# An LSTM with an adapter on one core: projection by quadrants, bias by matmuls, and the adapter's weight in 32 chained transfers

## The chip, the cores and the metric

One core of a Trainium2 chip runs the kernel. The metric is the device time of one execution in microseconds; three runs of the kernel before gave 603.7, 605.48 and 606.89, median 605.48.

## The reference

The input x has 16 sequences of 256 tokens with 256 features, all in 32-bit floats. An LSTM layer comes first, with residual:

```python
xz = einsum('ntd,dk->ntk', x, Wx) + b            # k = 4 gates of 256: i, f, o, g
z = xz_t + prev_h @ Wh                           # 256 steps, one after the other
next_c = sigmoid(f) * prev_c + sigmoid(i) * tanh(g)
next_h = sigmoid(o) * tanh(next_c)               # h0 = cond, c0 = 0
x = x + hs
```

Then an adapter, with residual, whose low-rank weights differ for each sequence and come from cond:

```python
c = layernorm(cond) * gamma + beta
h = gelu(c @ W1 + bias1)
w = h @ W2 + bias2                               # 16 x 8192; W2 is 256 x 8192, 8 MB
a1, b1, a2, b2 = split(w)                        # each 16 x 256 x 8
mid = gelu(x @ base_down + (x . a2) . b2)
out = x + mid @ base_up.T + (mid . b1) . a1
```

## The kernel before

Time is cut into 32 blocks of 8 steps. A block is 128 tokens (16 sequences by 8 steps), which fill the 128 partitions. For each block SP loads x (`load_x`), TensorE transposes it (`transpose_x`), ScalarE copies it to SBUF times two (`evacuate_x`), TensorE multiplies it with Wx in eight pieces (`project`: four column quarters of 256, two halves of the contraction), VectorE adds the bias on the way from PSUM to `proj` (`evacuate_projection`), and four SP DMAs move `proj` to `seed` (`load_seed`), so that the four quadrants of 32 partitions each hold a quarter of the hidden units for the 16 sequences, for every step of the block. This runs two blocks ahead of the recurrence.

A step: ScalarE copies the seeds into the PSUM banks z0, z1 and z_o (`seed_bank`, `seed_o`); TensorE adds h times Wh, with the 16 sequences as weights, four quadrants side by side (line 677); VectorE turns 32 by 32 blocks, ScalarE takes tanh, VectorE forms the cell and the hidden state, which is already transposed and is the next step's stationary operand. In the gaps TensorE does the projection of block k + 2 and the adapter of the block before.

Up to block 2 a planner by step, `make_weights`, puts the making of the adapter's weights between: W1 and the transposes of base_up in steps 2 to 5 of block 0, then W2 in 16 pieces, one a step from step `W_FIRST` = 7 on (line 606), its result added to bias2 by VectorE (line 882) and spread by POOL's DMAs (`place_w`, line 975) to w_tmp, b_t and a_t, of which w_tmp is transposed (line 618) in block 2. W2 is loaded in four transfers of 2 MB into three tiles (`load_w2`, line 276): the first at the start, two in block 0, the last in block 1, when its tile is free. bias2 is loaded by POOL, broadcast to 16 partitions in each quadrant.

Each engine works in program order and waits on semaphores. SP's order matters here: a DMA that stands behind a wait is not issued before the wait ends. In the projection before, the columns go gate by gate, so that one evacuation holds one gate for all quadrants, and a seed DMA, which takes one quadrant, needs all four. The bias b is spread to all partitions at the start by one-row matmuls (line 634); four matmuls on zeros run before (line 625).

Of the kernel before, what the change touches and what calls it, by code (L numbers as in the profile page):

```python
# [20 lines left out]
ALU = mybir.AluOpType  # L21
ACT = mybir.ActivationFunctionType
# [3 lines left out]
G = 4  # L26
P = 128
# [14 lines left out]
W_FIRST = 7  # L42
# [12 lines left out]
WARM_UP = 4  # L55


def lstm_adapter(nc, x, cond, Wx, Wh, b, base_up, base_down, gamma, beta, W1, bias1, W2, bias2, out):
    ctx = ExitStack()
    with ctx:  # L60
# [6 lines left out]
        def sem(name):  # L67
# [5 lines left out]
        ones = sb("ones", [P, P])  # L73
# [3 lines left out]
        b_row = sb("b_row", [1, G * H])  # L77
# [23 lines left out]
        w2 = {q: w2_tiles[n % 3] for n, q in enumerate(QUARTERS)}  # L101
        w_bias = sb("w_bias", [P, 4, W_COLS])
# [39 lines left out]
        consts_made = sem("consts_made")  # L142
        zeroed = sem("zeroed")
        w_loaded = {n: sem(f"{n}_loaded") for n in
                    ("wx_if", "wx_og", "wh", "b", "down", "up", "ln", "cond", "w1")}
        w2_loaded = [sem(f"w2_loaded{q}") for q in range(4)]
        w_bias_zeroed, w_bias_loaded = sem("w_bias_zeroed"), sem("w_bias_loaded")
# [38 lines left out]

        def gate_cols(t, gate):

            quadrants = t[:, :].rearrange("p (j n) -> p j n", n=ZW)
            if gate == 2:  # L190
                return quadrants[:, :, NM * GC:ZW].rearrange("p j (m c) -> p m j c", c=C)
            place = {0: 0, 1: 1, 3: 2}[gate]
            return quadrants[:, :, 0:NM * GC].rearrange("p j (m g c) -> p g m j c", m=NM, c=C)[:, place]
# [48 lines left out]
        def _(sp):  # L242
# [6 lines left out]
            def load_seed(f):  # L249
# [23 lines left out]
            w2_q = W2.rearrange("(k p) (q n) -> q p k n", p=P, q=4)  # L273
# [5 lines left out]
            sp.dma_start(b_row[:, :], b.rearrange("(a n) -> a n", a=1)).then_inc(w_loaded["b"], 16)  # L279
            load_cols(wx, Wx, 0, 0, 2 * H, "wx_if")  # L280
            load_cols(wx, Wx, 2 * H, 2 * H, 2 * H, "wx_og")
            sp.dma_start(c_in[:, :], cond).then_inc(w_loaded["cond"], 16)
            load_cols(wh, Wh, 2 * H, 3 * H, H, "wh")
            load_cols(wh, Wh, 0, 0, 2 * H, "wh")
            load_cols(wh, Wh, 3 * H, 2 * H, H, "wh")
# [9 lines left out]
            load_w2(QUARTERS[0])  # L295
# [30 lines left out]
        def _(act):  # L326


            act.wait_ge(zeroed, 1)
# [10 lines left out]
            def seed_bank(buf, s, m):  # L340

                act.activation(z_bank[m][:, 0:GC], seed[buf][:, s, GC * m:GC * (m + 1)], ACT.Copy)\  # L342
                   .then_inc(seeded[m], 1)

            def seed_o(buf, s):
                act.activation(o_bank[:, 0:OC], seed[buf][:, s, NM * GC:ZW], ACT.Copy).then_inc(seeded_o, 1)  # L346
# [14 lines left out]

            def make_weights(k, s):
# [11 lines left out]
                if k == 2 and s in (0, 4):  # L374
# [5 lines left out]
            def double_g(t, lo, ready):  # L380
# [628 lines left out]
```

## Time and profile before

| | |
|---|---|
| median of three runs | 605.48 us |
| profiled execution | 607.91 us, span of its instructions 605.7 |
| TensorE busy | 586.7 us (97%) |
| VectorE, ScalarE, GpSimd busy | 83%, 63%, 8% |
| mean granted TensorE clock | 0.994 |
| DMA | 39.74 MB, mean 66 GB/s |

The span is the time from the first to the last instruction of one profiled execution; the run's own time is 2.2 us longer. PE is TensorE, PEld its loading of weights, DVE VectorE, ACT ScalarE, POOL GpSimd, SP the engine that issues most DMAs. A 32-bit matmul of the program shows as two instructions. The spans of matmuls overlap, since they are pipelined: the distance of two starts says more than a duration.

### The profile page before, as it was taken

Reading aid. Unit: us, or ns where it says so; the run is one execution under the profiler, and the core shown is the slowest. Engines: PE = TensorE matmul, PEld = TensorE weight load, DVE = VectorE, ACT = ScalarE, POOL = GpSimd, SP = SyncE. Lnnn points to the kernel's source line nnn. Section 1 sums busy time; section 2 is a strip of 40 time slices with the busy share of each in tenths; the row PEclk is TensorE's granted clock in tenths of the full one; section 3 lists DMA queues with packets and bytes.
Section 4 is the critical chain, followed back from the end, with each engine's and each line's share of the span. In section 5 each row is a group of like instructions: output and inputs, shape, how many; then the busy total and the mean of one; then the engine's idle time right before and its main releaser. Section 6 shows DMA issues by size and latency. Waiting matters only on the chain.

```text
span 605.7 us, 34198 instructions
## 1 busy us (share of the span) xinstructions
PE 586.7 (97%) x14092; PEld 437.7 (72%) x14092; DVE 501.5 (83%) x2805; ACT 384.6 (63%) x2154; POOL 49.7 (8%) x96
## 2 busy tenths in 40 slices
PE   8698999999999999999999999999999999999997
PEld 5564567777777777777777777777777777777885
DVE  2577888888888888888888888888888888888873
ACT  1365566666666666666666666666666666666673
POOL 5001320000000000000000000000000000000000
PEclk9799999999999999999999999999999999999999
DMA  7889340232323113233311232322133233113201
GB/s 193 218 219 311 68 56 15 36 55 56 56 56 52 32 31 56 55 56 56 56 32 28 56 55 56 55 47 39 29 57 55 55 56 53 34 30 45 56 21 29
DMA packets 32142, 39.74 MB, mean 66 GB/s; under 512 B 3906, under 2 KB 29810, under 8 KB 30963
## 3 DMA queue, kind: packets, MB, share of 16 engines
q1 hardware_dynamic: 31282, 36.51, 30.3%
q8 instruction: 112, 1.84, 1.4%
q0 software_dynamic: 704, 1.05, 1.2%
q14 instruction: 44, 0.35, 0.2%
HBM read 16.05 MB, written 4.19 MB: 33 GB/s over the span
## 4 chain that ended last, share of the span: by engine, by line
PE 95%; issue 1%; DMA 1%; DVE 1%; POOL 1%; SPq 0%; ACT 0%; POOLq 0%; ACTq 0%
PE z L677 36%; PE x_bank L481 19%; PE z_o L677 9%; PE aux L507 8%; PE out_bank L531 7%; PE aux L492 3%; PE aux L459 3%; PE out_bank L563 2%; PE aux L514 2%; PE out_bank L606 1%; DMA seed<-proj 1%; PE out_bank L552 1%; PE x_bank L552 1%; DMA x_nat<-in_x 0%; PE x_bank L507 0%
## 5 line engine op out<-in xcount | busy, mean ns | idle before, releaser
L677 PE MATMUL z<-wh,h_t 128*16 128x96 f32 x8160 | 235.3, 249 | 3.5 <-issue 3.1
L677 PEld LDWEIGHTS z<-wh,h_t 128*16 128x16 f32 x8160 | 153.2, 96 | 109.5 <-DVE h_t L855 79.6
L830 DVE STREAM_TRANSPOSE z<-z 128x96 f32<-128x96 f32 x512 | 152.8, 299 | 73.3 <-PE z L677 47.6
L404 ACT ACTIVATE gates<-z 128x48 f32<-128x48 f32 x512 | 108.1, 211 | 122.6 <-DVE z L830 122.3
L481 PE MATMUL x_bank<-wx,x_t 128*128 128x256 f32 x512 | 156.3, 393 | 0.5 <-ACT x_t L336 0.5
L342 ACT ACTIVATE z<-seed 128x96 f32<-128x96 f32 x512 | 127.0, 248 | 5.8 <-DMA seed<-proj 5.8
L677 PE MATMUL z_o<-wh,h_t 128*16 128x64 f32 x4080 | 104.9, 219 | 0.1
L840 DVE SCALAR_TENSOR_TENSOR prod<-gates 128x32 f32<-128x32 f32 x512 | 98.7, 193 | 0.0
L481 PEld LDWEIGHTS x_bank<-wx,x_t 128*128 128x128 f32 x512 | 81.3, 197 | 5.9 <-issue 1.5
L677 PEld LDWEIGHTS z_o<-wh,h_t 128*16 128x16 f32 x4080 | 80.0, 97 | 0.6 <-issue 0.5
L346 ACT ACTIVATE z_o<-seed 128x64 f32<-128x64 f32 x256 | 58.4, 228 | 19.3
L952 POOL TENSOR_TENSOR xp<-x_t,h_t 128x128 f32<-128x128 f32 x60 | 30.4, 530 | 483.2 <-DVE h_t L855 449.1
L410 ACT ACTIVATE gate_o<-z_o 128x32 f32<-128x32 f32 x256 | 50.6, 198 | 27.1 <-DVE z_o L834 1.7
L834 DVE STREAM_TRANSPOSE z_o<-z_o 128x64 f32<-128x64 f32 x256 | 65.9, 257 | 0.2
L416 ACT ACTIVATE z_o<-z 128x16 f32<-128x16 f32 x256 | 43.0, 168 | 25.8 <-DVE z L845 0.4
L766 DVE TENSOR_TENSOR proj<-x_bank,b_all 128x256 f32<-128x256 f32 x128 | 54.1, 422 | 6.2 <-PE x_bank L481 6.0
L845 DVE SCALAR_TENSOR_TENSOR z<-prod 128x16 f32<-128x16 f32 x256 | 46.7, 182 | 8.7
L850 DVE SCALAR_TENSOR_TENSOR gates<-prod 128x32 f32<-128x32 f32 x256 | 47.2, 185 | 0.0
L416 ACT ACTIVATE tanc<-tanc 128x16 f32<-128x16 f32 x256 | 45.6, 178 | 0.2
L855 DVE SCALAR_TENSOR_TENSOR h_t<-gate_o,z_o 128x16 f32<-128x16 f32 x256 | 43.7, 171 | 0.2
L855 DVE SCALAR_TENSOR_TENSOR h_t<-gate_o,tanc 128x16 f32<-128x16 f32 x256 | 43.7, 171 | 0.0
L507 PE MATMUL aux<-xp,down 128*128 128x128 f32 x232 | 43.3, 289 | 0.0
(125 smaller groups left out, 518.9 us busy)
## 6 DMA issues: line engine op xcount, KB each, us to landing
seed<-proj SPq DMA_DIRECT2D x128, 128.0 KB, 4.4
w<-in_L_cond_W SPq DMA_DIRECT2D x4, 2048.0 KB, 10.6
x_nat<-in_x SPq DMA_DIRECT2D x32, 128.0 KB, 4.3
out<-y_nat SPq DMA_DIRECT2D x32, 128.0 KB, 4.2
wx<-in_L_cond_Wx SPq DMA_DIRECT2D x2, 512.0 KB, 4.9
wh<-in_L_cond_Wh SPq DMA_DIRECT2D x2, 256.0 KB, 6.6
wh<-in_L_cond_Wh SPq DMA_DIRECT2D x1, 512.0 KB, 5.8
w_bias<-in_L_cond_bias POOLq DMA_DIRECT2D x4, 128.0 KB, 6.8
```

Source lines behind the costliest of these rows:

```text
L342: act.activation(z_bank[m][:, 0:GC], seed[buf][:, s, GC * m:GC * (m + 1)], ACT.Copy)\
L346: act.activation(o_bank[:, 0:OC], seed[buf][:, s, NM * GC:ZW], ACT.Copy).then_inc(seeded_o, 1)
L404: act.activation(gates[s % 2][m][:, 0:3 * B].rearrange("p (g b) -> p g b", b=B), zt[m].rearrange("p (g c) -> p g c", c=C)[:, :, 0:B], ACT. ...
L416: act.activation(tanc[m], cell[m], ACT.Tanh, scale=0.5).then_inc(tanc_ready[m], 1)
L481: ins = pe.matmul(x_bank[q % 2][:, 0:XW], x_t[f.k % N_X][:, kc, :], wx[:, kc, q * XW:(q + 1) * XW], start=(kc == 0), stop=(kc == 1))
L507: ins = pe.matmul(mid_bank[a.lane][:, cols], lhs, rhs, start=(part == 0), stop=(part == 2))
L677: ins = pe.matmul(dst, h_prev[:, kc, :], rhs, start=False, stop=(kc == 1), skip_group_check=True)
L766: dve.tensor_tensor(gate_cols(proj[f.par], q), x_bank[q % 2][:, 0:XW].rearrange(units, m=NM, c=C), b_all[:, q * XW:(q + 1) * XW].rearrange ...
L830: dve.transpose(zt[m], z_bank[m][:, 0:GC]).then_inc(turned[m], 1)
L834: dve.transpose(zt_o, o_bank[:, 0:OC]).then_inc(turned_o, 1)
L840: dve.scalar_tensor_tensor(prod[m][:, :], now[:, 0:2 * B], 1.0, now[:, 2 * B:4 * B], ALU.add, ALU.mult).then_inc(prod_ready[m], 1)
L855: dve.scalar_tensor_tensor(h_t[k.par][:, m, s, 0:B], gate_o[:, B * m:B * (m + 1)], 1.0, tanc[m], ALU.add, ALU.mult).then_inc(ht_ready[m], 1)
```

## The change

The projection's columns now go by quadrant: piece q holds the four gates of quadrant q, `seed` has the order (m, gate, unit), the evacuation writes in one run, and a seed DMA needs only its own quarter. Wx and Wh are loaded by gates (g first, then i and f, then o). The bias b is spread by eight matmuls with a stationary operand of 128 rows of which only the first is not zero (it holds 2 or 4), from `b_pad`, which is zero below its first row; b and cond are loaded from ScalarE's queue. Six matmuls on zeros stand at the start instead of four, and one more after the transposes of cond. The whole projection of block 1 now comes ahead of step 0.

bias2 goes to one partition in each quadrant of the zeroed `bias_pad` (four DMAs on SP); TensorE spreads it to 16 partitions by matmuls (`spread_bias`: once before step 0, then in steps 0, 1 and 3), and ScalarE copies it (`keep_bias`). W2 is loaded in 16 pieces, each in two halves of 64 partitions, 256 KB each, and each half waits for the same half of the piece before. Everything that hangs on W2 moves two steps later (`W_FIRST` = 9); `place_w` and the waits for it move as well.

```diff
-W_FIRST = 7
+W_FIRST = 9
-WARM_UP = 4
+WARM_UP = 6
...
-                sp.wait_ge(xz_ready, f.k * XQ + XQ)
                 for j in range(NQ):
+                    sp.wait_ge(xz_ready, f.k * XQ + (j + 1))
                     sp.dma_start(seed[f.par][32 * j:32 * j + B, :, :], proj[f.par][:, ZW * j:ZW * (j + 1)])\
                       .then_inc(seed_loaded[f.par], 16)
...
-            def load_w2(q):
-                sp.dma_start(w2[q][:, :, :], w2_q[q]).then_inc(w2_loaded[q], 16)
+            def load_w2(piece):
+                n, i = divmod(piece, NQ)
+                q, (h, kc) = QUARTERS[n], divmod(i, 2)
+                if piece == 3 * NQ:
+                    sp.wait_ge(w_psum, 2)
+                for r, rows in enumerate((slice(0, P // 2), slice(P // 2, P))):
+                    if piece > 0:
+                        sp.wait_ge(w2_loaded[QUARTERS[(piece - 1) // NQ]][(piece - 1) % NQ][r], 16)
+                    sp.dma_start(w2[q][rows, kc, :].rearrange("p (j h n) -> p h j n", j=NQ, n=W_HALF)[:, h],
+                                 w2_parts[q, h, kc, rows]).then_inc(w2_loaded[q][i][r], 16)
...
+            bias_j = bias2.rearrange("(q j n) -> j q n", q=4, j=NQ)
+            sp.wait_ge(bias_zeroed, 1)
+            for j in range(NQ):
+                sp.dma_start(bias_pad[32 * j:32 * j + 1, :, :], bias_j[j:j + 1]).then_inc(bias_loaded, 16)
             load_seed(Blk(0, 0))
...
-            load_w2(QUARTERS[0])
             load_seed(Blk(0, 1))
             load_cols(down, base_down, 0, 0, D, "down")
             def one_block(k, front):
+                if not k.at_least(1):
+                    load_w2(0)
+                    load_w2(1)
                 if k.plus(3).exists():
                     load_x(k.plus(3))
-                if not k.at_least(1):
-                    load_w2(QUARTERS[1])
-                if k.k == 1:
-                    sp.wait_ge(w_psum, 2)
-                    load_w2(QUARTERS[3])
+                for piece in {0: range(2, 7), 1: range(7, 13), 2: range(13, 4 * NQ)}.get(k.k, ()):
+                    load_w2(piece)
                 if front:
                     load_seed(k.plus(2))
-                if not k.at_least(1):
-                    load_w2(QUARTERS[2])
...
+            def keep_bias(n):
+                act.wait_ge(bias_psum, n + 1)
+                act.activation(w_bias[:, QUARTERS[n], :], out_bank[:, :], ACT.Copy).then_inc(bias_ready, 1)
...
-                    ins = pe.matmul(x_bank[q % 2][:, 0:XW], x_t[f.k % N_X][:, kc, :], wx[:, kc, q * XW:(q + 1) * XW],
+                    ins = pe.matmul(x_bank[q % 2][:, 0:XW].rearrange("p (m g c) -> p m g c", m=NM, c=C),
+                                    x_t[f.k % N_X][:, kc, :],
+                                    wx[:, kc, :].rearrange("p (g m j c) -> p j m g c", g=G, m=NM, c=C)[:, q],
                                     start=(kc == 0), stop=(kc == 1))
...
+            def spread_bias(n):
+                if n == 0:
+                    pe.wait_ge(b_ready, 1)
+                    pe.wait_ge(bias_rows_made, 1)
+                    pe.wait_ge(bias_loaded, 16 * NQ)
+                else:
+                    pe.wait_ge(bias_ready, n)
+                for j in range(NQ):
+                    ins = pe.matmul(out_bank[32 * j:32 * j + B, :], row_of_quadrant[:, j, :],
+                                    bias_pad[:, QUARTERS[n], :], start=True, stop=True)
+                ins.then_inc(bias_psum, 1)
             def make_weights(k, s):
+                if k == 0 and s in (0, 1, 3):
+                    spread_bias((1, 2, None, 3)[s])
...
-                    if i == 0:
-                        pe.wait_ge(w2_loaded[q], 16)
+                    for half in w2_loaded[q][i]:
+                        pe.wait_ge(half, 16)
...
             transpose_x(Blk(0, 0), both)
-            pe.wait_ge(w_loaded["b"], 16)
-            for i, bank in enumerate((out_bank, x_bank[1])):
-                pe.matmul(bank[:, :], ones[0:1, :], b_row[0:1, i * 2 * H:(i + 1) * 2 * H],
-                          start=True, stop=True).then_inc(b_psum, 1)
-            project(Blk(0, 0), range(N_PIECES))
             pe.wait_ge(w_loaded["cond"], 16)
             for m in both:
-                ins = pe.transpose(out_bank[:, m * B:(m + 1) * B], c_in[:, m * P:(m + 1) * P], ident[0:B, 0:B])
+                ins = pe.transpose(x_bank[1][:, m * B:(m + 1) * B], c_in[:, m * P:(m + 1) * P], ident[0:B, 0:B])
             ins.then_inc(h0_psum, 1)
+            pe.matmul(o_bank[:, 0:GC], zeros[:, :], zeros[:, 0:GC], start=True, stop=True).then_inc(bits_set, 1)
+            pe.wait_ge(rows_made, 2)
+            pe.wait_ge(w_loaded["b"], 16)
+            for i, bank in enumerate((out_bank, tanc_bank)):
+                for place, gate in enumerate((0, 1, 3, 2)):
+                    quarters = bank[:, :].rearrange("p (j m g c) -> p g j m c", j=2, m=NM, c=C)
+                    ins = pe.matmul(quarters[:, place], rows_of[4 if gate == 3 else 2][:, :],
+                                    b_pad[:, gate * H:(gate + 1) * H]
+                                    .rearrange("p (m j c) -> p j m c", m=NM, c=C)[:, 2 * i:2 * i + 2],
+                                    start=(place == 0), stop=True, skip_group_check=True)
+                ins.then_inc(b_psum, 1)
+            project(Blk(0, 0), range(N_PIECES))
+            spread_bias(0)
             transpose_x(Blk(0, 1), both)
-            project(Blk(0, 1), range(N_PIECES // 2))
+            project(Blk(0, 1), range(N_PIECES))
...
             def one_block(k, front):
                 add_h(k)
-                if k.k in (0, 1):
-                    place_w(2 * k.k)
-                    place_w(2 * k.k + 1)
+                for n in {0: (0,), 1: (1, 2), 2: (3,)}.get(k.k, ()):
+                    place_w(n)
```

## Rows read from the trace of the kernel before

**Rows 1.** Chain of work that ended last, its share by engine.

```profile
PE 95%; issue 1%; DMA 1%; DVE 1%; POOL 1%; SPq 0%; ACT 0%; POOLq 0%; ACTq 0%
```

**Rows 2.** Timeline of TensorE, block 4: start, duration, line, operands, count.

```profile
104.25 0.86 PE L677 MATMUL z<-wh,h_t 128*16 128x96 f32 x32
104.93 0.41 PE L677 MATMUL z_o<-wh,h_t 128*16 128x64 f32 x16
105.27 0.71 PE L507 MATMUL aux<-xp,down 128*128 128x128 f32 x4
...
106.36 0.96 PE L677 MATMUL z<-wh,h_t 128*16 128x96 f32 x32
```

**Rows 3.** Timeline of TensorE: steps 0, 8, 16, 24, 25, 32 and 40.

```profile
22.18 1.48 PE L677 MATMUL z<-wh,h_first 128*16 128x96 f32 x32 [4.65 <-ACT z L342]
...
43.43 0.33 PE L677 MATMUL z<-wh,h_t 128*16 128x96 f32 x2
...
65.04 0.84 PE L677 MATMUL z<-wh,h_t 128*16 128x96 f32 x32
...
83.30 0.94 PE L677 MATMUL z<-wh,h_t 128*16 128x96 f32 x32 [0.23 <-DVE h_t L855]
...
85.47 0.68 PE L492 MATMUL aux<-xp,a_w 128*128 128x128 f32 x4 [1.00 <-POOL xp L952]
...
86.52 0.85 PE L677 MATMUL z<-wh,h_t 128*16 128x96 f32 x32
...
101.95 0.95 PE L677 MATMUL z<-wh,h_t 128*16 128x96 f32 x32
...
119.56 0.96 PE L677 MATMUL z<-wh,h_t 128*16 128x96 f32 x32
```

**Rows 4.** Chain of waits, first 31 us: start, duration, what.

```profile
0.74 2.70 DMA x_nat<-in_x
...
7.94 6.54 PE x_bank L481 x16
...
14.50 0.43 DVE proj L766
...
15.02 0.64 SPq L258
...
17.00 4.70 DMA seed<-proj
```

**Rows 5.** Timeline of TensorE, bias matmuls and the second projection.

```profile
4.17 2.07 PE L634 MATMUL out_bank<-b_row,ones 1*128 1x512 f32 x2
...
15.53 1.99 PE L481 MATMUL x_bank<-wx,x_t 128*128 128x256 f32 x8 [0.47 <-ACT x_t L336]
```

**Rows 6.** Stretches: us, engines' busy time, granted clock, DMA share, GB/s.

```profile
8.00:10.00 2.00, 2.00 (x5) 1.64 (x6) 0.73 (x2) 0.42 (x1) 1.43 (x3) 1.00 1.08 393
...
22.00:24.00 2.00, 1.82 (x48) 1.67 (x48) 0.58 (x3) 0.71 (x5) 0.00 (x0) 0.50 1.17 407
```

**Rows 7.** Chain of waits, 50 to 62 us.

```profile
53.07 1.38 issue
...
59.42 1.68 issue
```

**Rows 8.** DMA queues and issues; stretches 44 to 60, 32 to 38 and 570 to 600.

```profile
q8 instruction: 3, 0.05, 1.2%
...
down<-in_L_cond_base_down SPq DMA_DIRECT2D x1, 256.0 KB, 5.4
...
out<-y_nat SPq DMA_DIRECT2D x5, 128.0 KB, 2.3
```

**Rows 9.** Timelines of TensorE and ScalarE: W1, one W2 piece, the doubling of Wx.

```profile
32.33 1.07 PE L580 MATMUL aux<-c_t,w 128*128 128x16 f32 x8
...
45.37 0.63 PE L606 MATMUL out_bank<-w,hid 128*16 128x256 f32 x8
...
7.79 0.63 ACT L381 ACTIVATE wx<-wx 128x512 f32<-128x512 f32 x1 [3.13 <-DMA wx<-in_L_cond_Wx]
```

More of the change, by code:

```diff
@@ L72, in lstm_adapter @@
         zeros = sb("zeros", [P, P])
-        ones = sb("ones", [P, P])
+        rows_of = {n: sb(f"row_{n}", [P, P]) for n in (2, 4)}
         gelu_0 = sb("gelu_0", [1, 1])
@@ L326, in _ @@
         def _(act):
+            act.dma_start(c_in[:, :], cond).then_inc(w_loaded["cond"], 16)
+            act.wait_ge(b_zeroed, 1)
+            act.dma_start(b_pad[0:1, :], b.rearrange("(a n) -> a n", a=1)).then_inc(w_loaded["b"], 16)
             act.wait_ge(zeroed, 1)
@@ L373, in make_weights @@
                     act.activation(up_t[:, s - 4, :], out_bank[:, 0:D], ACT.Copy).then_inc(up_ready, 1)
-                if k == 2 and s in (0, 4):
+                if k == 0 and s in (0, 1, 3):
+                    keep_bias((1, 2, None, 3)[s])
+                if k == 2 and s in (1, 5):
                     n = s // 4
@@ L430, in one_block @@
                         seed_o(ahead.par, s_next)
-                    if s == 0 and not k.at_least(1):
+                    if s == 1 and not k.at_least(1):
                         evacuate_x(k.plus(2))
-                    if not k.at_least(EARLY + 1):
+                    if not k.at_least(EARLY + 2):
                         make_weights(k.k, s)
@@ L500, in down_full @@
                     if i == 0:
-                        pe.wait_ge(w_placed[3], W_PLACED)
                         pe.wait_ge(w_loaded["down"], 16)
                         pe.wait_ge(u_ready[a.lane], a.seq.k + 1)
+                    if i == 2 and a.blk.k == EARLY:
+                        pe.wait_ge(w_placed[3], W_PLACED)
                     cols = slice(l * P, (l + 1) * P)
@@ L525, in up_full @@
                         pe.wait_ge(up_ready, 2)
+                        if a.blk.k == EARLY:
+                            pe.wait_ge(w_biased, 4 * NQ // 2)
+                        pe.wait_ge(v_ready[a.lane], a.seq.k + 1)
+                    if i == 2 and a.blk.k == EARLY:
                         pe.wait_ge(w_placed[0], W_PLACED)
-                        pe.wait_ge(v_ready[a.lane], a.seq.k + 1)
                     cols = slice(m * P, (m + 1) * P)
@@ L565, in transpose_y @@
                     ins.then_inc(y_psum[a.lane], 1)
+            def spread_bias(n):
[9 more added lines that the diff above has]
+                ins.then_inc(bias_psum, 1)
             def make_weights(k, s):
+                if k == 0 and s in (0, 1, 3):
+                    spread_bias((1, 2, None, 3)[s])
                 if k == 0 and s == 2:
@@ L609, in make_weights @@
                         ins.then_inc(w_psum, 1)
-                if k == 2 and s in (0, 4):
+                if k == 2 and s in (1, 5):
                     n = s // 4
@@ L717, in one_block @@
                         if not k.at_least(1):
-                            if s == 0:
+                            if s == 1:
                                 transpose_x(f, both)
-                            if s < 2:
-                                project(Blk(0, 1), range(4 + 2 * s, 6 + 2 * s))
                         project(f, range(pieces[s], pieces[s + 1]))
-                    if not k.at_least(EARLY + 1):
+                    if not k.at_least(EARLY + 2):
                         make_weights(k.k, s)
@@ L821, in _ @@
             dve.tensor_scalar(c_stat[:, 3:4], c_stat[:, 2:3], 1.0 / D, LN_EPS, ALU.mult, ALU.add).then_inc(ln_step, 1)
-            for q in range(2):
+            for q in range(XQ):
                 evacuate_projection(Blk(0, 1), q)
@@ L871, in make_weights @@
                        .then_inc(cond_t_ready, 1)
-                if k > 0 and s % 2 == 0:
-                    u = ((k - 1) * TB + s) // 2
+                u, between = divmod(k * TB + s - W_FIRST - 1, 2)
+                if 0 <= u < 2 * NQ and not between:
                     n, h = divmod(u, 2)
@@ L917, in one_block @@
                         add_residual(done)
-                    if not k.at_least(1) and s < 2:
-                        evacuate_projection(Blk(0, 1), 2 + s)
                     if front and k.at_least(1) and s in EVACUATE_AT:
@@ L925, in one_block @@
                         evacuate_projection(f, max(0, s - 4))
-                    if not k.at_least(EARLY + 1):
+                    if not k.at_least(EARLY + 2):
                         make_weights(k.k, s)
@@ L955, in add_h @@
                         .then_inc(xp_ready, 1)
+            pool.memset(bias_pad[:, :, :], 0.0).then_inc(bias_zeroed, 1)
             for i in range(2):
                 pool.memset(seed[i][:, :, :], 0.0).then_inc(seeds_zeroed, 1)
-            pool.memset(w_bias[:, :, :], 0.0).then_inc(w_bias_zeroed, 1)
-            pool.wait_ge(w_bias_zeroed, 1)
-            bias_q = bias2.rearrange("(q j n) -> j q n", q=4, j=NQ)
-            for j in range(NQ):
-                pool.dma_start(w_bias[32 * j:32 * j + B, :, :], bias_q[j].partition_broadcast(B))\
-                    .then_inc(w_bias_loaded, 16)
             pool.wait_ge(ln_step, 6)
```

107 lines of the change are left out of this document (55 added, 52 removed).

## The prediction

> **What bounds the kernel now.** I read the chain of waits first, then the TensorE timeline of a late step, then the steps of the first four blocks, then the DMA issues. The chain lies on TensorE for 95% [rows 1], but that does not make TensorE's matmuls the price of a step. One step of block 4 takes 106.36 - 104.25 = 2.11 us [rows 2], its eight 17.6 [rows 3]; z, z_o, four matmuls for the adapter and one piece of the projection stand one behind the other, and the next z starts when the new h is there [rows 2]. So from step 25 on every step is 2.2 us, and what the change can move lies ahead: the start (step 0 begins at 22.18) and blocks 0 to 3, which take 21.25, 21.61, 18.26 and 18.65 us where 17.6 is the pace [rows 3]. Up to step 25 at 86.52 that is 64.3 us for 25 steps, against 55 at 2.2 a step.
>
> **The late steps.** The projection's matmuls keep 256 columns, but read them in eight runs of 32 instead of one run. The z matmuls read three such runs: 32 of them, four side by side, take 0.68 us, 85 ns a group, and z_o's 16 with two runs 0.34, also 85 ns [rows 2]. A third run costs nothing that shows, so I take 0 for the late blocks. Bounds: -1 us (VectorE now writes the result in one run) to +3 us (12 ns for each of two projection matmuls in 30 blocks of 8 steps, half of it hidden).
>
> **The start.** Before: x lands 2.70 us after 0.74, four one-row bias matmuls run from 4.17 to 7.94, sixteen projection matmuls take 6.54 us, 0.41 each, the last VectorE copy ends at 14.93, and four seed DMAs are issued only then, the last at 17.00, landing 4.70 us later [rows 4, 5]. Eight of the same matmuls at 15.53 took 1.99 us with the tail of the last, about 0.22 apart [rows 5]. That is half of 0.41, so the sixteen ran mostly at TensorE's lower level of 1.2 GHz, although the granted clock reads 1.00 there; it reads 0.50 from 22 to 24, after TensorE had stood still from 17.5 to 22.2 [rows 6]. The first steps pay for that too.
>
> After: two more warm-up matmuls, the c_in transposes and a filler push the bias matmuls to about 5.0. They cover the same 1024 columns, 3.8 us at the lower level and 1.9 at the upper [rows 5], but with all 128 rows, and nothing stands between them and the projection. ScalarE's wait for the last of Wx ended at 7.79 [rows 9]; b leaves SP's queue ahead of it, so I take 7.4, and the projection starts between 7.6 and 8.5. It takes 3.5 us at the upper level and 6.8 at the lower. Ends of the two: 11.2 and 15.3. I take 11.8, nearer to the upper level, since TensorE is now busy from 1.06 on without a pause, and from 5.0 on with full matmuls, which before began only at 7.87. Then, on TensorE: the first bias2 spread, two groups of four at 512 columns, 0.86 (W2's two of 256 columns take 0.63 with the tail [rows 9], 0.43 at 0.22 each); two x transposes 0.45; a gap of 0.85 in which ScalarE copies the bias (0.63, as its copy of 512 columns [rows 9]) and x; the whole second projection 3.5. Step 0 at 11.8 + 5.7 = 17.5.
>
> The seeds are the second path: one quarter is issued as soon as it is copied, so only the last is late: 11.8 + 0.7 for the copy + 0.1 + 3.4 to 4.7 + 0.45 for ScalarE = 16.5 to 17.8, level with TensorE's path. The gain at step 0 is 22.2 - 17.5 = 4.7 us. Moved issues: the four bias2 DMAs leave POOL for SP, ahead of the seeds; at 0.6 us each, as a seed's issue [rows 4], SP is through with them at about 8.6, and the first seed is not ready before 9.1, so they are hidden; bare, they would cost up to 2.4. b and c_in go to ScalarE's queue, where nothing waits before the copy of x at 4.5.
>
> **Blocks 0 to 3 if nothing is late.** Block 0: the rest of the second projection leaves steps 0 and 1, bias spreads of 0.86 come into steps 0, 1 and 3. Around z and z_o (1.24) a step has about 0.95 free. Step 0 holds; step 1 has 0.3 too much with the x transposes; step 3 has the spread and eight W1 matmuls (1.07 [rows 9]), 0.9 too much; W2 leaves step 7. I take 19.0 for 21.25. Block 1: two stops of 1.38 and 1.68 us stand in the middle of z matmuls that wait for nothing, "issue" in the chain [rows 7]. At that time SP's 2 MB transfers of W2 are in flight, and the fetches of instructions (q8) use the same DMA engines [rows 8]; I read the stops as late fetches. Transfers of 256 KB, of which two are in flight, should not hold them up: 17.8 for 21.61. If they stay, +3. Block 2: 18.3 as before; the two extra w_tmp transposes only move by a step. Step 24: POOL placed a_t ahead of xp and TensorE stood 1.00 us for it [rows 3]; the order is turned, but W2's last piece is now in this step: 2.6 for 3.22. Step 25 at 17.5 + 19.0 + 17.8 + 18.3 + 2.6 = 75.2, which is 11.3 earlier.
>
> **W2 in a chain: the new wait.** W2 is 16 pieces of two halves; SP waits for a half of the piece before, and only then issues the same half of the next. What SP holds behind such a wait are x loads and seeds. Piece n is used at the end of step 9 + n. The period: an undisturbed load of 128 KB landed in 2.70 [rows 4]; 128 KB more at the 393 GB/s of the weight loads [rows 6] adds 0.33; SP wakes 0.1 after a release (14.93 to 15.02 [rows 4]). That is 3.15. Fetches of 16 KB (three in 16 us at 1.2% of 16 engines [rows 8], so 1 us each on one engine) will hit some halves: I estimate 0.2 a period, 3.35 in all. Ends: 2.7 (a store of 128 KB took 2.3 [rows 8], so 2.3 + 0.33 + 0.1) and 5.5 (256 KB behind seeds took 5.4 [rows 8]). I stay near the 2.70, the only load with nothing ahead of it.
>
> From T0 = 17.5: the first piece is issued at T0 + 1.9, lands at +5.3, then pieces 1 to 6 a period each, the sixth issued at +22. Now SP issues four seeds and an x load; from the first seed's issue to the last's landing took 6.7 us [rows 4], and piece 7 waits in the rings behind them: landed at +32. Piece 12 is issued at +45.4, the next four seeds and x follow, piece 13 lands at +55.1, 14 at +59, 15 at +62.4. Needed without delay: piece 7 at +38.5, 13 at +52.3, 15 at about +57. So the chain is early until piece 12 and late by some 2.8, 1.5 and 1.1 us at the last three, 5.3 together. Step 25 then begins at T0 + 63 = 80.5, 6.0 us earlier than 86.52. The x load of block 2 (landing at +54) and the seeds of block 3 (+53.3) are needed at +54.5 and +55: just in time.
>
> The Trainium skill's page "DMA: Bandwidth & Descriptors", section "Rules for kernel authors", speaks against this edit: it wants one transfer of 128 partitions and 1 MiB or more, and says that two over disjoint partition halves serialise on the same 16 engines. No row here shows two half loads side by side. If the rule held fully, each half would land with both moved, a period would be 0.66 longer, and the sum 599.5 + 12 x 0.66 = 607.4, the same within 0.5%; the third rival is this and more.
>
> **Sum.** Profiled execution: span 605.7, 607.9 with what lies around it, 2.4 above the median of 605.48. Step 25 at 80.5 for 86.52, late steps 0: span 599.7, and with the same difference taken off the median 605.48 - 6.0 = 599.5.
>
> **Rivals.** (1) The chain is never late. At a period of 2.9 or less, pieces 13 to 15 arrive in time and all 11.3 us stay: 594.2. For it: the store's 2.3; against: seeds and fetches in the same rings. By the same skill page, section "Anatomy of one DMA", a transfer costs an estimated 2.0 us + bytes / 436 GB/s, 2.6 for 256 KB, which would give this outcome.
> (2) TensorE stays at the lower level through the projection, as it did before, so the warming does not do what it says: bias to 8.5, projection to about 14.5, step 0 at 20.2. The chain starts later by as much: 599.5 + 2.75 = 602.2. For it: in the sixteen matmuls before it came late; against: those bias matmuls had one row.
> (3) Slower: the chain of W2 becomes the bound of steps 16 to 25. At a period of 4.3, midway between 3.15 and the end of 5.5, the twelve periods that follow each other cost 12 x 0.95 = 11.4 more: step 25 at 91.9, 610.9. It decides from 3.85 on, where the 6.0 us are used up. TensorE would stand 2 us and more at the end of steps from 16 on, and might fall to the lower level. Against: the 5.4 stood behind seeds, as only pieces 0, 7 and 13 do here.
>
> **Chances.** Forecast 0.49, rival 1 0.18, rival 2 0.15, rival 3 0.13, the rest 0.05. 0.5% is 3.0 us, about what a measurement of this kernel can tell from none (the three runs lie 3.2 apart). Faster: 0.45 of the forecast, rival 1, 0.10 of rival 2 and 0.01 of the rest, 0.74. Same: 0.04, 0.05 of rival 2, 0.04 of the rest, 0.13. Slower: 0.13. The range takes in rivals 1 and 2 and the cost of a stop that stays or of slower late steps: 593.5 to 606.
>
> **What would show it.** Right: step 0 near 17.5, projection matmuls about 0.22 apart before 11, no "issue" stops between 40 and 62, waits of TensorE on w at steps 22 to 24 only, step 25 near 80, steps of 2.2 after. Wrong: W2 halves that take 4 us and more from issue to landing, waits on w from step 16 on, a granted clock of 0.50 after step 0, or late steps that are not 2.2.

## The result, and the profile after

The changed kernel takes 619.5 us (median of four runs, 618.37 to 624.47); the kernel before, on the same chip, 606.18. The ratio is 1.024, 95% interval 1.0173 to 1.0307: slower, where 599.5 was forecast. The third rival came true, and more of it than its 610.9. The profiled execution is the longest of the four, 624.47 us with a span of 622.7, so its trace shows some 5 us more than the median has.

The first row that differs is the chain of waits by engine: against [rows 1] TensorE has lost 7 points, and DMA has gone from 1 to 7, all of them W2's.

```profile
PE 88%; DMA 7%; DVE 2%; SPq 1%; issue 1%; POOL 0%; ACT 0%; POOLq 0%
```

TensorE's timeline at steps 0, 8, 16, 24 and 25, to be laid beside [rows 3] (start, duration, line, operands, count):

```profile
17.43 0.85 PE L723 MATMUL z<-wh,h_first 128*16 128x96 f32 x32
...
36.42 0.96 PE L723 MATMUL z<-wh,h_t 128*16 128x96 f32 x32 [0.22 <-DVE h_t L903]
...
61.55 1.16 PE L723 MATMUL z<-wh,h_t 128*16 128x96 f32 x32
...
96.56 0.83 PE L723 MATMUL z<-wh,h_t 128*16 128x96 f32 x32
...
102.41 0.85 PE L723 MATMUL z<-wh,h_t 128*16 128x96 f32 x32
```

Step 0 stands at 17.43 (22.18 before), block 0 takes 18.99 (21.25), block 1 25.13 (21.61), block 2 35.01 (18.26), and step 25 comes at 102.41, 15.9 later than before. From there to the end of the span it takes 520.3 us, for 519.2 before, and a late step beside [rows 2] shows 2.10 us from z to z, the projection's strided columns included.

```profile
121.46 0.85 PE L723 MATMUL z<-wh,h_t 128*16 128x96 f32 x32
122.13 0.41 PE L723 MATMUL z_o<-wh,h_t 128*16 128x64 f32 x16
122.47 0.71 PE L525 MATMUL aux<-xp,down 128*128 128x128 f32 x4
...
123.56 0.63 PE L723 MATMUL z<-wh,h_t 128*16 128x96 f32 x16
```

So the loss has its place: blocks 1 and 2. TensorE's waits there, by what ended them (total us, times, longest; "issue" means that no wait shows):

```profile
PE out_bank L643 <- DMA w<-in_L_cond_W: 15.0, 6, 4.8
```

Six stops on W2, 15.0 us together, at pieces 9 to 13 and 15 (piece 14 lands just as TensorE gets to it). A seventh stop, before step 16, is for the x of block 4, the first load of SP's block 1; SP's own timeline says why, and below it TensorE's row:

```profile
30.10 19.20 SPq L280 DMA_DIRECT2D w<-in_L_cond_W  x10
49.48 3.57 SPq L254 DMA_DIRECT2D seed<-proj  x4
53.09 0.60 SPq L243 DMA_DIRECT2D x_nat<-in_x  x1
```

```profile
59.25 0.69 PE L477 MATMUL aux<-ident,x_nat 128*128 128x128 f32 x2 [5.92 <-DMA x_nat<-in_x]
```

SP spends 19.20 us on ten halves of W2, each behind a wait, then issues the seeds, and only then the x load; TensorE stands 5.92 us for it. What releases SP is in the chain of waits, 60 to 103 us (start, duration, what): one W2 landing after another, but for 79.84 to 85.14, where SP issues block 3's seeds and an x load, and TensorE behind the last.

```profile
60.78 4.78 DMA w<-in_L_cond_W
...
65.57 5.78 DMA w<-in_L_cond_W
...
71.37 3.94 DMA w<-in_L_cond_W
...
75.32 4.52 DMA w<-in_L_cond_W
...
85.14 6.50 DMA w<-in_L_cond_W
...
91.65 4.10 DMA w<-in_L_cond_W
...
95.76 6.08 DMA w<-in_L_cond_W
101.84 0.14 issue
101.98 0.62 PE out_bank L643 x8
```

The page's list of DMA issues gives the median from issue to landing (KB each, us; W1 is the thirty-third), and the stretches (as [rows 6]) the clock: 0.50 is 1.2 GHz, and TensorE had just stood 4.84 us for piece 13 (its row comes last).

```profile
w<-in_L_cond_W SPq DMA_DIRECT2D x33, 256.0 KB, 4.2
```

```profile
54.00:60.00 6.00, 0.75 (x3) 0.75 (x4) 0.72 (x5) 1.12 (x8) 0.52 (x2) 0.61 1.00 146
...
90.00:96.00 6.00, 4.23 (x64) 2.94 (x68) 2.29 (x11) 1.52 (x9) 0.50 (x2) 0.50 0.37 94
```

```profile
91.77 1.05 PE L643 MATMUL out_bank<-w,hid 128*16 128x256 f32 x8 [4.84 <-DMA w<-in_L_cond_W]
```

What the change was meant to remove is gone: of the "issue" stops of 1.38 and 1.68 us [rows 7] this much is left in the chain:

```profile
22.73 0.25 issue
...
44.08 0.17 issue
```

### The profile page after: what moved, and what is told of

Read it like the earlier page. It is cut to its first block, busy times and chain, and to the rows that moved or that the text cites. A ratio compares the mean times of both kernels' runs of the same rounds, so it can differ in the third digit from the quotient of the medians.

```text
span 622.7 us, 34326 instructions
## 1 busy us (share of the span) xinstructions
PE 591.3 (95%) x14142; PEld 443.2 (71%) x14142; DVE 504.0 (81%) x2810; ACT 386.3 (62%) x2158; POOL 47.4 (8%) x91
## 4 chain that ended last, share of the span: by engine, by line
PE 88%; DMA 7%; DVE 2%; SPq 1%; issue 1%; POOL 0%; ACT 0%; POOLq 0%
PE z L723 33%; PE x_bank L496 17%; PE z_o L723 9%; PE aux L525 8%; DMA w<-in_L_cond_W 7%; PE out_bank L552 7%; PE aux L509 3%; PE aux L477 2%; PE out_bank L584 2%; PE aux L532 2%; SPq L254 1%; PE out_bank L573 1%; PE x_bank L573 1%; PE out_bank L597 0%; PE x_bank L525 0%
## 5 line engine op out<-in xcount | busy, mean ns | idle before, releaser
L723 PEld LDWEIGHTS z<-wh,h_t 128*16 128x16 f32 x8160 | 155.5, 96 | 107.2 <-DVE h_t L903 78.8
L496 PE MATMUL x_bank<-wx,x_t 128*128 128x256 f32 x512 | 154.5, 389 | 0.6 <-ACT x_t L344 0.6
L496 PEld LDWEIGHTS x_bank<-wx,x_t 128*128 128x128 f32 x512 | 80.0, 194 | 3.9 <-ACT x_t L344 0.8
```

Source lines behind the costliest of these rows:

```text
L496: ins = pe.matmul(x_bank[q % 2][:, 0:XW].rearrange("p (m g c) -> p m g c", m=NM, c=C), x_t[f.k % N_X][:, kc, :], wx[:, kc, :].rearrange("p ...
L723: ins = pe.matmul(dst, h_prev[:, kc, :], rhs, start=False, stop=(kc == 1), skip_group_check=True)
```

## The experiments

The theories, with the numbers that the expectations use: (1) W2's chain is too slow, since each piece waits for a whole landing; (2) x and seeds are late because SP holds them behind the chain's waits; (3) W2 in 32 transfers is slow as such; (4) the "issue" stops are late instruction fetches, behind whatever else is in flight. Two more on the 4.2 us: (5) the runs of 1 KB, (6) the latency of a transfer or its sharing. T0 is the start of step 0. Ratios are to the kernel before on the same chip.

**e2_unchained: the waits of the chain taken out, and nothing else.**

```diff
-                    if piece > 0:
-                        sp.wait_ge(w2_loaded[QUARTERS[(piece - 1) // NQ]][(piece - 1) % NQ][r], 16)
```

> The change, without SP's wait for the half before: the same 32 transfers of 256 KB in the same order. Theory 1 (it is the wait for each landing, some 4.2 us for 256 KB, that makes W2 late): W2 lands in some 25 us of transfer, no wait on w, 595 to 601, the seeds and x loads behind it later than in the chain. Theory 3 (it is the form, runs of 1 KB in transfers of half the partitions, that is slow): W2 lands hardly earlier than in the chain, 612 to 620.

Measured: 611.88 us, 1.0047 (1.0018 to 1.0076). No wait on w is left, so the 32 transfers are not slow as such, and theory 3 falls, though the time comes near its 612; most of the loss goes with the waits. Theory 1's 595 to 601 is missed as well. But "issue" stops of 10.4 us come in their place, the longest 3.96. The stretches between them, cut at the stops (TensorE's matmuls are the first x), are the finding of this run:

```profile
0.00:30.20 30.20, 27.82 (x344) 20.73 (x344) 18.55 (x74) 11.97 (x49) 6.54 (x11) 1.00 0.89 186
30.20:40.40 10.20, 7.47 (x126) 5.50 (x126) 5.22 (x31) 4.72 (x27) 0.00 (x0) 0.83 1.12 218
40.40:52.20 11.80, 9.45 (x251) 6.02 (x252) 8.29 (x46) 5.99 (x36) 1.01 (x2) 1.00 0.94 181
52.20:58.40 6.20, 4.66 (x126) 2.95 (x126) 4.33 (x23) 2.84 (x18) 0.11 (x1) 1.00 1.12 225
```

The stops come after matmul 344, 470, 722 and 848: always a multiple of 126 apart (with one record missing from the third stretch), whatever the matmul is.

**e1_whole: W2 in four transfers of 2 MB at the places of before; all else as changed.**

```diff
+            def load_w2(q):
+                sp.dma_start(w2[q][:, :, :], w2_q[q]).then_inc(w2_loaded[q], 16)
...
```

> The change, with W2 in the four transfers of 2 MB and at the places of SP's queue as before. If W2's chain alone costs (theory 1), the start's gain of 4.7 us and part of block 0's stay and the late W2 goes: 597 to 601, step 25 near 80. If something else of the change costs as well (the bias2 spreads, place_w's order, the later W2), it stays above 606. The stops called issue may come back in block 1, up to 3 us.

Measured: 608.25 us, 1.0018 (0.9995 to 1.004). No wait on w, but a stop of 4.47 us after matmul 344, with the rings at 370 GB/s and the clock down behind it, and one of 2.06 after 722: 6.5 us, where up to 3 were expected. Step 0 stands at 19.27 and block 0 takes 25.29 us, so the start's gain is given back in one stop.

```profile
30.28 4.47 issue
...
52.22 2.06 issue
```

```profile
30.00:36.00 6.00, 1.53 (x29) 1.07 (x19) 1.26 (x7) 1.07 (x6) 0.00 (x0) 0.64 1.02 370
```

**e3_two_ahead: each half waits for the piece before the last, so four halves are in flight.**

```diff
-                    if piece > 0:
-                        sp.wait_ge(w2_loaded[QUARTERS[(piece - 1) // NQ]][(piece - 1) % NQ][r], 16)
+                    if piece > 1:
+                        sp.wait_ge(w2_loaded[QUARTERS[(piece - 2) // NQ]][(piece - 2) % NQ][r], 16)
```

> The change, each half waiting for the same half two pieces before, so that four transfers of 256 KB are in flight instead of two. Theory 1: a piece comes every 2.1 to 2.5 us instead of every 4.3, which keeps up with a step of 2.2: 594 to 600. Theory 3: the transfers share their rate, a piece still comes every 4 us, 615 to 620.

Measured: 606.56 us, 0.9975 (0.9939 to 1.0011). Halves land 1.2 us apart and 6.0 after their issue, by the medians; no wait on w, but stops of 2.75 us (after matmul 344) and 3.10 (after 1223 in the trace, where 1226 would be the next multiple: a few records are missing). Both theories miss the time; theory 1 is right that W2 is in time.

**e4_x_first: x loaded one block earlier, ahead of the chain; the chain as changed.**

```diff
-                if k.plus(3).exists():
-                    load_x(k.plus(3))
+                if not k.at_least(1):
+                    load_x(k.plus(3))
+                if k.plus(4).exists():
+                    load_x(k.plus(4))
```

> The change, with each x load one block earlier in SP's queue, so that x of block 4 is no longer held behind pieces 2 to 6 of W2. Theory 2 (the cost comes from x and seeds held behind the chain's waits): the stop of 5.9 us at step 15 goes and the time falls by 5 us and more, 613 or less. Theory 1: the stop goes, but W2's last pieces are late by as much more, 617 to 620.

Measured: 619.39 us, 1.0194 (1.0149 to 1.024). The stop on x is gone and the time stays: TensorE waits 16.5 us for w (longest 5.4), and 3.62 us at step 16 for an h that hangs on block 2's seeds. These stand behind the chain too (ScalarE waits 4.3 us for them; in the changed kernel they land at 58.41, just ahead of that x), so this run takes away one half of theory 2 only. Theory 2 names real stops, and the one taken away cost nothing while the chain ends later. e5, e7, e9 and e13 to e16 keep this edit.

**e5, e7 and e9: how many halves are in flight, and where.** e5 allows three; e7 two at pieces 1, 2, 7 and 13, next to seeds, and four elsewhere; e9 is e5 with pieces 13 and 14 issued ahead of block 3's seeds.

In this order, e5's and e7's lines for the half or piece that is waited for, and e9's groups:

```diff
+                    half = 2 * piece + r - 3
...
+                    back = piece - (1 if piece in (1, 2, 7, 13) else 2)
...
-                for piece in {0: range(2, 7), 1: range(7, 13), 2: range(13, 4 * NQ)}.get(k.k, ()):
+                for piece in {0: range(2, 7), 1: range(7, 15), 2: range(15, 4 * NQ)}.get(k.k, ()):
```

> The change with three transfers of 256 KB in flight instead of two (each half waits for the third before it) and each x load one block earlier. Theory 1: a piece every 2.9 us instead of 4.3, W2's last piece some 15 us earlier than in the change, waits on w of 0 to 4 us; with theory 4 (the stops called issue are late fetches of instructions, behind what is in flight) the stops stay under 1 us, as with two: 597 to 603. Against theory 4: stops of 3 us at the same matmuls as with four in flight, 604 to 608.

> The change with each x load one block earlier and the half before as what is waited for in pieces 1, 2, 7 and 13 (next to the seeds), two pieces before elsewhere. Theory 4: the two stops of 2.8 and 3.1 us, which came with four in flight beside seeds and x, go or shrink under 1 us, and W2 still comes in time: 598 to 603. If the stops hang on four in flight alone they come back at other places: 604 to 608.

> The change with three transfers of 256 KB in flight, each x load one block earlier, and pieces 13 and 14 ahead of block 3's seeds in SP's queue. With three in flight the only large stops were 1.4 and 3.1 us of waiting for pieces 13 and 14 behind these seeds. If the seeds' 5 us in the rings are what delays them (theory 2 in this place), they go: 598 to 601. If W2 is late there by its rate alone, the wait moves to other pieces: 603 to 606.

Measured: e5 605.03 us, 0.9966 (0.9951 to 0.9981); e7 604.52, 0.9953 (0.9934 to 0.9972); e9 606.45, 0.9981 (0.9965 to 0.9997), where block 3's seeds come late by 3.4 us and a wait on w of 2.1 stays. None reached its better outcome. TensorE's waits in e5, then in e7:

```profile
PE out_bank L646 <- DMA w<-in_L_cond_W: 4.5, 2, 3.1
PE z_o L726 <- issue: 1.1, 1, 1.1
```

```profile
PE z_o L726 <- issue: 2.7, 2, 2.3
PE z L726 <- issue: 1.8, 3, 0.8
```

Three in flight still wait for w and hardly for instructions, four the other way round. e7 beats both kernels, by 0.3 to 0.7% of the one before; its interval overlaps that of e5.

**e6_runs_4k: halves of the same 256 KB as 64 rows of 4 KB runs, not 1 KB.**

```diff
-            w2_parts = W2.rearrange("(k p) (q j h n) -> q h k p j n", p=P, q=4, j=NQ, n=W_HALF)
+            w2_parts = W2.rearrange("(k p) (q c n) -> q k c p n", p=P, q=4, c=2)
...
```

> The change, with each transfer of 256 KB cut out of W2 as 64 rows of 4 KB in one run (half the columns of a quarter) instead of four runs of 1 KB a row; TensorE waits for both halves of the columns at the first use, so W2 is needed up to two steps earlier. Theory 5 (a landing of 4.2 us holds one us for the 256 runs): 3.1 to 3.4 us from issue to landing where nothing is ahead. Theory 6 (the landing is latency and sharing, whatever the runs): 4.0 to 4.4. The time itself says little: 610 to 620 by theory 5, 618 to 626 by theory 6.

Measured: 622.88 us, 1.0256 (1.0232 to 1.028). From issue to landing (least, median, most):

```profile
DMA to landing us min/median/max: 3.3/3.8/7.6
```

0.4 less than 4.2, where theory 5 wanted about 1.0 and theory 6 nothing: the runs are part of it. SP's own time to issue is 0.13 of the 0.4 (0.47 us for 0.60). That the kernel is no faster fits W2 being needed earlier, as expected; TensorE waits 17.8 us for it.

**e12_serial_quarter: one half in flight.** As e10, below, but each half waits for the one just before.

```diff
...
+                    half = 2 * piece + r - 1
...
```

> As e10 (only pieces 0 to 3 are loaded, and these four serve for all sixteen, which leaves out part of the computation), but each half waits for the half just before it, so that one is in flight at a time. If the 4.2 us from issue to landing come from sharing the 16 DMA engines with the other half, a half alone lands in 3.1 to 3.3 us. If they are a half's own (latency and the tail of its slowest engine), it lands in 3.6 to 4.0 all the same. The time: eight halves at about 3.9 us are 31 us, and piece 3 is used at the end of step 12, 28 us after step 0; so waits on w of 0 to 6 us, 597 to 603.

Measured: 603.39 us in one run. In its chain, three of the six landings that had no seeds beside them (3.33 to 3.82, middle 3.55):

```profile
29.89 3.68 DMA w<-in_L_cond_W
...
37.43 3.46 DMA w<-in_L_cond_W
...
44.43 3.33 DMA w<-in_L_cond_W
```

Between the two expectations: some 0.5 over the 3.03 (2.70 + 0.33) of the prediction is a half's own. For the other half's share e10 is the like, with the same halves and two in flight. The lists of DMA issues for the third to the seventh half (KB each, median us to landing), e12, then e10:

```profile
w<-in_L_cond_W SPq DMA_DIRECT2D x5, 256.0 KB, 3.5
```

```profile
w<-in_L_cond_W SPq DMA_DIRECT2D x5, 256.0 KB, 3.7
```

So 0.2 here; in the changed kernel, e4 and e8 the same five halves have medians of 4.1, 3.9 and 4.2, which makes 0.4 to 0.6. Against one run with one half in flight, the other half's share is 0.2 to 0.6, and what else stands between 3.5 and the 4.2 of all halves is open.

**e10 and e11: the change, and the kernel before, without W2's last 6 MB.** The first quarter serves for all four. e10's edit; e11 leaves out three of the four loads in the same way.

```diff
-        w2 = {q: w2_tiles[n % 3] for n, q in enumerate(QUARTERS)}
+        w2 = {q: w2_tiles[0] for q in QUARTERS}
-                for piece in {0: range(2, 7), 1: range(7, 13), 2: range(13, 4 * NQ)}.get(k.k, ()):
+                for piece in {0: range(2, 4)}.get(k.k, ()):
...
```

> The change with the first quarter of W2 alone loaded (pieces 0 to 3 in the chain) and used for all four quarters, so that 6 MB of the 8 are left out. It shows what the rest of the change is worth with no W2 in the rings. Theories 1 and 4: no waits on w, no stops, steps of 2.2 from block 1 on: 594 to 597. If the spreads, place_w's order or the later W2 steps cost something of their own, 599 and more.

> The kernel before with the first quarter of W2 alone loaded (one transfer of 2 MB) and used for all four, 6 MB left out. Theory 4 (the stops called issue are fetches of instructions behind W2's transfers): the stops of 1.4 and 1.7 us in block 1 and most of the 0.7 us at step 7 go, 3 to 4 us less than before: 603 to 604.5. If the stops belong to the instructions or their place and not to W2's traffic, they stay: 606.5 to 608.

Measured: e10 598.15 us, 0.9846 (0.9814 to 0.9878), e11 601.46, 0.9905 (0.9875 to 0.9935). All that is left of TensorE's "issue" stops and waits on DMA in e10:

```profile
PE z L723 <- issue: 0.4, 1, 0.4
```

e10 falls between its two expectations, e11 gains more than was expected. So W2's last 6 MB cost the kernel before 0.0095, some 5.8 us (3.4 of them are "issue" stops in the traces, 3.8 before for 0.4 in e11; the clock stayed up behind them), and the changed one 21 by the medians (619.5 - 598.15, on two chips) and 24 by the ratios; the rest of the change is worth 3.3 us between these two.

**e8_one_row: the bias matmuls of the start on one row, as before the change.**

```diff
-                    ins = pe.matmul(quarters[:, place], rows_of[4 if gate == 3 else 2][:, :],
+                    ins = pe.matmul(quarters[:, place], rows_of[4 if gate == 3 else 2][0:1, :],
-                                    b_pad[:, gate * H:(gate + 1) * H]
+                                    b_pad[0:1, gate * H:(gate + 1) * H]
```

> The change, with the eight matmuls for b on one row instead of 128, of which 127 are zero. If the full rows are what brings TensorE to its upper level before the projection, the projection's matmuls are 0.43 us apart at the start and step 0 begins at 18.5 to 21 instead of 17.4. If it is the time in which TensorE is busy, whatever the rows, the projection runs 0.22 apart from its first third on and step 0 begins at 17.4 to 18.

Measured: 624.76 us in one run. Its timeline, and that of the changed kernel, at the second eight bias matmuls and the projection:

```profile
7.16 1.91 PE L678 MATMUL tanc<-b_pad,row 1*128 1x128 f32 x8
8.99 6.07 PE L496 MATMUL x_bank<-wx,x_t 128*128 128x256 f32 x16
```

```profile
7.01 1.33 PE L678 MATMUL tanc<-b_pad,row 128*128 128x128 f32 x8
8.18 3.62 PE L496 MATMUL x_bank<-wx,x_t 128*128 128x256 f32 x16
```

The same columns, but behind one-row matmuls the level does not rise before some 13.8, and step 0's z stands at 20.69, 3.3 later; behind full rows it has risen within the second eight. The levels are read from the distance of the matmuls; the granted clock reads 1.00 in both stretches, as it did before.

**e13 to e16: W2's load fitted to the gaps.** e13 sets the number in flight by place; e14 issues 2 MB without waits ahead of the seeds of block 1 and the rest by place; e15 and e16 1 MB, with four and with three in flight at most.

e13's line first, then e14's:

```diff
+                    half = 2 * piece + r - {1: 2, 2: 2, 7: 2, 8: 3, 9: 3, 10: 3, 11: 3, 12: 3, 13: 2}.get(piece, 4)
...
+                    half = 2 * piece + r - {4: 2, 5: 3, 6: 4, 7: 4, 8: 4, 9: 2, 10: 2}.get(piece, 3)
...
+            for piece in range(4):
+                load_w2(piece)
             load_seed(Blk(0, 1))
```

> x loads one block earlier, and the chain's wait by place: two halves in flight at pieces 1, 2, 7 and 13, which share the rings with seeds and x, three at pieces 8 to 12, four elsewhere. Theories 1 and 4 together (the loss is the rate of the chain, and what limits the rate is the instruction fetch behind it): no or one short wait on w (under 2 us in all), issue stops under 2 us, 599 to 602, ratio 0.985 to 0.993. If four in flight hold up the fetches whatever stands beside them: issue stops of 2 to 4 us as in e3, 603 to 606, ratio 0.994 to 1.000.

> Pieces 0 to 3 (2 MB) are issued without waits behind up_raw and ahead of the seeds of block 1; pieces 4 to 9 in block 0, 10 to 15 in block 1, all ahead of the seeds of block 3; x one block earlier; in flight: two halves at pieces 4, 9 and 10, which stand next to seeds, four at 6 to 8, three elsewhere. If the loss is only the chain's rate against the fetches behind it: the last piece lands before 70 and is used at 76, no wait on w over 0.5 us, issue stops under 1.5 us in all, step 0 still at 17.5 to 18.2, 598 to 601, ratio 0.984 to 0.991. If three and four in flight hold up the fetches also away from seeds: issue stops of 2 to 5 us with a fall of the clock, 603 to 606. If the 2 MB ahead of the seeds of block 1 make these late, block 0 is longer than 20.

> As e14, but only pieces 0 and 1 (1 MB) ahead of the seeds of block 1, pieces 2 to 7 in block 0, 8 to 15 in block 1; in flight: two halves at 2, 7, 8 and 9, four at 4 to 6, three elsewhere. If e14's stop came from the heap of 2 MB, seeds, base_down and x: the fetch that is due at 24 ends before 28.5, no stop over 1 us, block 0 takes 19.0 to 19.6, the last piece lands before 75, 598 to 602, ratio 0.984 to 0.993. If the late fetch only moves: one or two stops of 2 us and more with the clock at 0.5 behind them, 603 to 607.

> As e15, but never more than three halves in flight behind the first 1 MB (two at 2, 3, 7, 8 and 9). If what is in flight sets the stops: the same or fewer stops than e15, the pieces 3 to 6 about 1 us later each, and waits on w of 0 to 3 us at pieces 14 and 15: 599 to 603. Against e15 it tells whether four in flight away from seeds cost a stop.

Measured: e13 605.05 us, 0.9977 (0.9953 to 1.0001); e14 608.44, 1.002 (1.0 to 1.004); e15 611.49, 1.0088 (1.0057 to 1.012); e16 614.2, 1.0121 (1.0087 to 1.0154). None reached its better outcome. e13 has one "issue" stop of 2.4 us and one wait on w of 3.3. e14 has no wait on w, and its one large stop is again the one after matmul 344; behind it the clock is down (0.68 from 34 to 40 us):

```profile
34.52 0.62 PE L725 MATMUL z_o<-wh,h_t 128*16 128x64 f32 x12 [4.94 <-issue]
```

```profile
34.00:40.00 6.00, 5.30 (x78) 3.76 (x78) 2.67 (x18) 2.35 (x13) 0.00 (x0) 0.68 0.81 170
```

The halves moved ahead pushed the seeds of block 1, base_down and two x loads back onto the next fetch. In e15 that stop is 3.57 us, behind one of 1.7 at 25, and e16, with at most three in flight, has the same two (3.3 and 1.8), so four in flight away from seeds are not what makes them. At 81 e15 has a new one: block 3's seeds stood behind piece 15 in SP's queue, and TensorE waited 8.3 us for the h that hung on them.

```profile
PE z L725 <- DVE h_t L905: 9.1, 4, 8.3
PE z_o L725 <- issue: 3.6, 1, 3.6
```

## Why the prediction was wrong

**The start: right.** Step 0 at 17.43 for 17.5. The first eight bias matmuls ran at the lower level (5.18 to about 7.2), within the second eight it rose, and the projection took 3.62 for 3.5. The last seed landed at 16.63, which with ScalarE's 0.45 makes 17.1 for 16.5 to 17.8. e8 bears out, in one run, the reason that was given, full rows ahead of the projection.

**Blocks 0 to 3 without a late W2, and the fetch stops: right.** 18.99 for 19.0 in block 0; the two stops left with the 2 MB transfers, as foretold for two halves in flight, and e1 brings stops back. e10, where W2 is never late, gives blocks 0 to 2 and step 24: 19.13, 17.82, 18.37 and 2.62 us, for 19.0, 17.8, 18.3 and 2.6. Some luck is in block 0: its working takes 1.24 us for z and z_o, which [rows 2] put at 1.02.

**The late steps: right.** 2.10 for 2.11; a third run of columns costs nothing that shows.

**The chain of W2: the step that failed.** The term that was mis-sized is the period: "That is 3.15. Fetches of 16 KB [...] will hit some halves: I estimate 0.2 a period, 3.35 in all", and then "I stay near the 2.70, the only load with nothing ahead of it" (its terms, 2.70 + 0.33 + 0.1, make 3.13). The periods measured 4.56 on average, and a half lands in 4.2 us by the median, for 3.03. Alone in e12 it already takes 3.5, 0.5 more than the 2.70 says; the other half, in flight at the same time, adds 0.2 to 0.6; the rest is open. By e6, 0.4 hang on the runs of 1 KB (x's tokens, too, are read in 1 KB, so the 2.70 did not warn of it, and why these cost more is open). A rival for the 0.5 stands untested: a half goes to 64 partitions, the x load to 128, and no run loads a piece over all 128.

The Trainium skill's page "DMA: Bandwidth & Descriptors", section "Rules for kernel authors", says that two halves serialise on the same engines; the prediction priced that at 0.66 a period and did not take it into the sum. The 0.2 to 0.6 above agree with some of it, and no run here shows all of it; with it alone the sum would have been 607.4, still too low. The same page's "Anatomy of one DMA", behind the prediction's 2.6, has its figures from transfers that GpSimd issues, and W2's are issued by SP; here the halves alone in e12 take 3.3 to 3.8, and the measurement decides.

**What it came to, by landings of the second half of each piece** (read from the trace after: piece 0 at 27.00, 6 at 52.66, 7 at 60.76, 12 at 84.17, 13 at 91.63, 15 at 101.84). The first lands at T0 + 9.6 where 5.3 was said: the seeds of block 1 and base_down stand in the rings (they land from 20.14 to 25.32), which the sum left out, though the third rival names piece 0 as behind seeds: +4.3. Thirteen periods have no seeds of SP's ahead of them; they take 4.56 on average, for 3.35: +15.7. The two behind seeds, pieces 7 and 13, take 8.10 and 7.46 for 6.6 and 6.35: +2.6. Together 22.6, and step 25 came 21.9 later than forecast (102.41 - 80.5; the forecast gave pieces 14 and 15 some 0.6 more than a period). The x stop lies inside that: the load was to be there before piece 7's +32 and is wanted at +35.9; it came at +41.8, and e4 shows that it cost nothing beside the chain. Block 2's seeds, late as well at +41.0, stand inside it too. So do the falls of the clock, which the third rival only said might come.

**The third rival: right in place, too small in price.** At its period of 4.3 it put step 25 at 91.9. The period was that within 0.3 and above its point of decision, 3.85, which no run tests; it kept the first piece at +5.3, and it took the twelve periods to start as early as forecast.

**Rival 1, the chain never late**, said 594.2. e10, where only four pieces are loaded, gives 598.15 against 607.17 on its chip, 9.0 less (9.3 by the ratio): near the 11.3 that all of the change without a late W2 was to bring.

**Where the gain went.** Two halves in flight move 512 KB in 4.2 us, 125 GB/s. From the first issue at 19.2 to about 74.4 (T0 + 57), 8.39 MB want 152. More in flight reach it (e3 and e7 without a wait on w, e5 with 4.5 us of it), and then TensorE stops for instructions. Between the two, e7 has the lowest ratio. That the stops are fetches is inferred, but the traces bear it out: their place in the count of matmuls, and the times of the packets of queue q8. At each of the 28 "issue" stops above 0.6 us in the traces kept, the last such packet ends 1.2 to 1.9 us before TensorE goes on, as in e14, where one ends at 33.1 and TensorE goes on at 34.5; and the stops go where the traffic goes (e10, e11). No run took the fetches away. A kernel in which the load of W2 costs nothing was not found.

## To carry to other kernels

Before a large load is cut into chained pieces, divide: bytes in flight by the landing time of such a piece with its like in flight, against bytes by the time until they are needed; here the rate came to 0.8 of what was needed, and the load cost over 20 us. What stands behind the chain's waits in the same queue (x loads, seeds) is late with it, and moving it ahead helps only when the chain itself is in time. To know what a load costs at all, take it, or most of it, out of both kernels: 6 and over 20 us here, which says that from the load at most some 6 us were to be had.

## What the runs showed of the hardware

That TensorE's instructions come in packets over the same DMA engines as the data is read from these numbers: 28,284 instructions (14,142 matmuls and as many loads of weights) and 112 packets of 16 KB of queue q8 on the page, 252 instructions or 126 matmuls to a packet, and all "issue" stops above 0.6 us, in every kernel here, fall on that count, but for up to four records that are missing. In e10, where little is in flight, the packets of the trace tell more: one ends 2.7 to 3.9 us after the boundary before it (the first eight), and the next boundary comes 4.6 to 6.0 us after that one; TensorE goes on 1.2 to 1.9 us behind a packet that is late. So, as an estimate, 2 us of other traffic ahead of it at most pass before TensorE stands, and four halves beside seeds, or 2 MB, are more.

The Trainium skill's page "Runtime: NRT & Kernel Launch", section "Instruction fetch mechanics", has blocks of 16 KiB, 256 instructions, fetched by the sequencer's own DMA queue while the block before is executed, at a cost "mostly hidden". The trace agrees on the size, and its times fit one block ahead; that it is hidden it contradicts with stops of up to 4.94 us where more was in flight.

Such stops also brought the clock down, and so cost more than their length. In e1, with its stop of 4.47 us, it reads 0.51 from 31.6 to 38.5, and block 0 takes 25.29 us for e10's 19.13, 6.16 more. Behind a stop of 2.31 us in e7 it reads 0.50, the first stretch below; behind the 1.68 of the kernel before 1.00, the second.

```profile
52.30:55.70 3.40, 3.40 (x58) 2.30 (x50) 2.26 (x14) 1.64 (x10) 0.00 (x0) 0.50 0.77 174
```

```profile
62.00:70.00 8.00, 8.00 (x200) 4.71 (x201) 7.52 (x41) 5.47 (x32) 3.10 (x6) 1.00 0.38 77
```
